# TensorE's warm-up in a table-lookup and ranking kernel: 56 one-column products and 10 of 512 columns instead of 13 of 512

## What is computed

```python
e = jnp.stack([tbl_0[ids[:, 0]], ..., tbl_25[ids[:, 25]]], axis=1)        # 512 x 26 x 128
combined = jnp.concatenate([dense[:, None, :], e], axis=1)                # 512 x 27 x 128
interactions = jnp.einsum('bnd,bmd->bnm', combined, combined)
z = jnp.concatenate([dense, interactions[:, _TRIU_I, _TRIU_J]], axis=1)   # 128 + 351
h = jnp.concatenate([z, dense], axis=1)
h = jnp.maximum(h @ W_top1 + b_top1, 0.0)                                 # 607 -> 512
h = jnp.maximum(h @ W_top2 + b_top2, 0.0)                                 # 512 -> 256
y = h @ W_top3                                                            # 256 -> 1
```

## Time and profile before

| what | before |
|---|---|
| runs, median (lowest to highest) | 102.37 us (102.18 to 102.53) |
| the profiled execution | 101.98 us |
| its span, first to last instruction | 100.2 us |
| PE busy | 94.5 us, 1525 products and 1525 weight loads |
| DVE / ACT / POOL busy | 53.2 / 48.1 / 60.5 us |
| the chain that ended last | PE 69%, DVE 20%, DMA 3%, ACT 3%, issue 2% |
| the warm-up, L474 | 13 products, 1.2 to 6.3 us |

### The profile page before, as it was taken

One profiled execution on the slowest core, in us unless ns is written; L12 is line 12 of the kernel. 1 busy time (PEld: TensorE's weight loads), 2 busy tenths in 40 slices (PEclk: granted clock), 3 DMA queues, 4 the chain that ended last, 5 costly groups with the idle time before them and its releaser, 6 DMA issues.

```text
span 100.2 us, 3476 instructions
## 1 busy us (share of the span) xinstructions
PE 94.5 (94%) x1525; PEld 78.4 (78%) x1525; DVE 53.2 (53%) x118; ACT 48.1 (48%) x82; POOL 60.5 (60%) x66
## 2 busy tenths in 40 slices
PE   5999997999999999999999999999999999998990
PEld 1358765778888888899989978899988979987970
DVE  4599999999999979927000250226002701026020
ACT  2844999299399579747310325006240444003521
POOL 1488777777777878767777777777777760000000
DMA  2899999999999999981212212122221220000000
GB/s 62 237 333 245 242 238 257 241 232 232 256 241 241 244 233 259 380 316 48 59 52 59 59 52 62 52 59 52 59 59 52 59 52 26 7 7 0 7 0 1
DMA packets 5365, 13.46 MB, mean 134 GB/s; under 512 B 1731, under 2 KB 1991, under 8 KB 5222
## 3 DMA queue, kind: packets, MB, share of 16 engines
q1 hardware_dynamic: 3260, 9.11, 35.4%
q0 software_dynamic: 1920, 3.94, 15.5%
q10 hardware_dynamic: 170, 0.18, 0.7%
HBM read 13.23 MB, written 0.00 MB: 132 GB/s over the span
## 4 chain that ended last, share of the span: by engine, by line
PE 69%; DVE 20%; DMA 3%; ACT 3%; issue 2%; DVEq 0%
PE ps_a L337 30%; DVE onehot L573 12%; PE ps_gram L374 12%; PE ps_a L423 9%; PE ps_h L437 5%; PE ps_rows L352 5%; DVE part_sb L582 4%; PE ps_a L400 3%; DMA idrow<-ids_by_table 3%; DVE table_sb L600 2%; DVE z L605 2%; PE ps_h L466 1%; PE ps_rows L449 1%; PE ps_z L385 1%; ACT xt L694 1%
## 5 line engine op out<-in xcount | busy, mean ns | idle before, releaser
L310 POOL DMA_INDIRECT rows_sb<-tbl,ids_sb x60 | 60.0, 1000 | 20.9 <-issue 16.8
L337 PE MATMUL ps_a<-onehot,part_sb 125*128 125x512 f32 (+1 forms) x208 | 45.0, 367 | 0.8 <-DVE part_sb L582 0.5
L337 PEld LDWEIGHTS ps_a<-onehot,part_sb 125*128 125x128 f32 x208 | 34.7, 190 | 7.9 <-DVE part_sb L582 1.7
L573 DVE TENSOR_SCALAR onehot<-idrow,row_id 125x1024 fp32r<-125x1024 int16 (+1 forms) x42 | 27.9, 716 | 2.2 <-DMA idrow<-ids_by_table 1.7
L582 DVE TENSOR_TENSOR part_sb<-table_sb,part_sb 125x512 fp32r<-125x512 f32 x22 | 14.4, 677 | 2.3 <-ACT part_sb L666 2.3
L687 ACT COPY xt<-ps_a 128x512 f32<-128x512 f32 (+1 forms) x13 | 7.5, 579 | 14.8 <-PE ps_a L337 14.8
L374 PE MATMUL ps_gram<-xt 128*27 128x27 f32 x1024 | 13.2, 195 | 0.3
L694 ACT COPY xt<-ps_rows 128x512 f32<-128x512 f32 (+3 forms) x17 | 9.9, 588 | 7.3 <-PE ps_rows L352 7.3
L374 PEld LDWEIGHTS ps_gram<-xt 128*27 128x27 f32 x1024 | 11.0, 107 | 3.0 <-ACT xt L694 0.6
L666 ACT CAST part_sb<-table_sb 125x1024 fp32r<-125x1024 f32 (+1 forms) x12 | 11.7, 984 | 2.7 <-DMA table_sb<-tbl 2.7
L636 DVE TENSOR_SCALAR table_sb<-ps_a,columns_sb 128x128 f32<-128x128 f32 x8 | 2.4, 346 | 18.9 <-PE ps_a L423 15.7
(11 more groups left out here) (41 smaller groups left out, 43.5 us busy)
## 6 DMA issues: line engine op xcount, KB each, us to landing
table_sb<-tbl SPq DMA_DIRECT2D x11, 448.0 KB
idrow<-ids_by_table SPq DMA_DIRECT2D x5, 256.0 KB, 8.5
w_sb<-w SPq DMA_DIRECT2D x1, 1280.0 KB, 11.9
rows_sb<-tbl,ids_sb POOLq DMA_INDIRECT x60, 6.6
table_sb<-tbl SPq DMA_DIRECT2D x10, 52.0 KB
w_sb<-w SPq DMA_DIRECT2D x1, 512.0 KB, 10.8
dense_sb<-dense_by_column SPq DMA_DIRECT2D x1, 256.0 KB, 9.0
idrow<-ids_by_table ACTq DMA_DIRECT2D x1, 128.0 KB, 2.9
```

The costliest lines, as they stand in the source:

```text
L310: pool.indirect_dma_start(rows_sb[:, t % ROWS_RING, k, :], None, tables[f], bass.IndirectOffsetOnAxis(ids_sb[:, t, f:f + 1], 0),).then_inc ...
L337: last = pe.matmul(ps_a[:, i % 2, a:b], parts_sb[part][:, w, c * D:(c + 1) * D], unit_onehot(u, c)[:, member, a:b], start=(part == HIGH an ...
L573: dve.tensor_scalar(unit_onehot(u, c), idrow[0:VP, w, 0:n, :], row_id[0:VP, first + c:first + c + 1], None, ALU.is_equal).then_inc(onehot_ ...
```

## The change

The warm-up constant becomes 10, and 56 products of one column on one column of weights are issued in front of it. Nothing else is changed: the lookups and all that follows stand 106 instructions later in TensorE's program (56 x 2 more, 3 x 2 fewer). The results of both loops are overwritten later, as before.

```diff
-WARM_UP = 13
+WARM_UP = 10
+SMALL = 56
...
             pe.wait_ge(zeros_ready, 1)
+            for _ in range(SMALL):
+                pe.matmul(ps_z[0:1, 0, 0:1], zeros[:, 0:1], zeros[:, 0:1], start=True, stop=True)
             for _ in range(WARM_UP):
                 pe.matmul(ps_z[:, 0, :], zeros[:, 0:P], zeros[:, :], start=True, stop=True)
```

## The result

The changed kernel takes 103.53 us in the median of 6 runs (102.56 to 104.08); the kernel before, run beside it on the same chip, takes 102.27 us (101.57 to 102.53). The ratio is 1.0118, with a 95% interval of 1.0076 to 1.016: slower by 1.2%, where the prediction had 101.8 us and called faster the likeliest. The profiled execution took 104.08 us, the longest of the six, for a span of 102.3 us.

What follows compares the result with a forecast made beforehand. VectorE was taken to bound the kernel until 20.40 us, then TensorE, with instruction-fetch stops late. Terms -0.73 + 0.10 + 0.05 = -0.58 us from the 102.37 us median gave 101.8 us, range 101.3 to 102.9; faster had 0.55.

Steps and rivals of the forecast that it cites:

- What bounds the kernel, and what a stop is: TensorE bounds from 20.40 us; it stops wherever it uses up a 256-instruction block faster than the next is fetched, 3.6 us.
- The 3.6 us that I called the measured minimum: At every block border: time from entering a block to the next being usable, 1.1 + 1.1 + 1.4 us.
- The stop among the L400 products: Between first and second L400 product, near 91 us: the 0.46 us stop goes, -0.73 us, bounds -0.46 and -0.84.
- The stop in the last gram stretch: Gram products from 87.82 us: a stop of 0.2 to 0.5 us instead of 0.28, +0.1, bounds -0.1 and +0.25.
- Earlier borders move into other stretches: Block borders from 50 to 80 us: each has more than 3.6 us in front, so no new stop, 0.
- the fixed delay from border to packet: At every block border: the next block's instruction packet starts about 1.1 us after TensorE enters the block.
- The fetch near 38 us: Instruction fetch amid table and weight transfers: ready by 48 us, before its block is wanted at 50; cost 0, bound +1.
- The warm-up: Before the first lookup: 56 small products at 33 ns, three large ones fewer, net +0.05 us, bounds 0 and +1.2.
- The 0.56 us that I let the clock give back: First lookup product, now starting as the clock level rises: no longer pays 0.56 us for the low level.
- Dear small products: Rival, before lookup 0: small products cost 55 ns each, lookup 0 ends 1.2 us later, result 102.9 us; chance 0.12.
- The clock rises later: Rival, first lookups: one-column products don't count as work, level rises at 8.9 us, +0.9 us, result 102.7; chance 0.15.
- The stop only moves: Rival: a border hits another short stretch or the late fetch holds gram up, taking back 0.5 to 0.7 us; chance 0.18.

Runs made afterwards that it cites:

- shifted by 192: Against the kernel before: 7 large and 102 small warm-up products instead of 13 large, +192 instructions for all that follows; 102.54 us, ratio 1.0037.
- shifted by 256: Against the kernel before: 5 large and 136 small warm-up products instead of 13 large, +256 instructions, one whole block; 103.34 us, ratio 1.012.

## Why the prediction was wrong

**What bounds the kernel, and what a stop is: held in kind, not in its number.** Blocks of 256 instructions in packets of 16 KB stand, and the stops after 85 us end at totals of 193 + 256 k in every kernel. The 3.6 us that I called the measured minimum is none. In the trace that I had, TensorE had executed 2443 products and loads, 2497 with the waits, by 84.96 us:

```profile
0.00:84.96 84.96, 82.28 (x1221) 67.82 (x1222) 49.61 (x103) 44.76 (x70) 60.45 (x66) 1.00 0.62 158
```

and it restarted at 2753 at 88.23, 3.27 us later. In the kernels shifted by 192 and 256 the block behind 2753 was in use 3.0 us after that border, with next to no stop (86.74 to 89.75 and 86.25 to 89.30 us, products 0.02 and 0.06 us apart at the crossing). The part that varies is the one from the border to the packet, which I took as 1.1 us throughout. That holds where TensorE has just restarted after a stop (1.1 to 1.2 us in the changed kernel and the one before). Elsewhere the packet starts mostly between 0.2 us before TensorE has executed the border (82.57 us for one executed at 82.81, with 53 small products behind the lookups) and 1.5 us after it, and in a few places over 2 us after it. From the start of a packet to use there are at least 2.2 us (87.19 to 89.40 with 64 small products, 87.53 to 89.75 shifted by 192). The Trainium skill ("Runtime: NRT & Kernel Launch", Instruction fetch mechanics) has crossing a block mostly hidden; late stops of 0.25 to 1.64 us in seven traces say otherwise where a block is used up by products 10 ns apart. The measurement decides.

**The stop among the L400 products, -0.73: held.** It went, and the products follow one another without a break. In the chain the four of them take 91.04 to 92.39 = 1.35 us before and 0.62 us after, which is 0.73 us less.

**The stop in the last gram stretch, "+0.1": too small.** I gave 0.2 to 0.5 us for it, counting 3.6 us from a border that TensorE passes at 85.3 to 85.6. The stop is 0.66 us, since that border itself was reached only at the end of another stop, at 87.86, and 87.86 + 3.8 = 91.68. Where the other stop is absent (64 small products) this one is 0.04 to 0.12 us in the chain, less than I gave, since 3.6 us was too long.

**"Earlier borders move into other stretches; from 50 to 80 us each has more than 3.6 us in front by my count … so 0": this step failed.** The count ended at 80 us, and the border that mattered lies behind it: what I called 2647 in the old program, whose block was asked for one block earlier, at old 2391, at 82.94 us. From there to 2647 are 4.9 us as it ran, and TensorE was ready after about 3.1 (at 86.03). By my own rule of 3.6 us that was a stop of 0.5 us, had I done the count. It was 1.64 because the packet left 2.2 us after its border and not 1.1: the second thing that the prediction had wrong is the fixed delay from border to packet. With the packet in time (64 small products; the last gathers left out) the stop is not there at all. The term of the sum is +1.6 instead of 0. What made the packet late is open. That the request waits while TensorE's program stands in a semaphore wait behind the border fits the changed kernel, its repetition and one place in the trace of before, where it costs nothing (the border at 59.65 us, a wait passed at 60.3, the packet at 61.46); it doesn't fit the border 449 of that same trace, or the packets that were in time with the same waits behind them.

**The fetch near 38 us, 0: held.** It moved at 42 us, the stretch from 50 us on starts at 49.97 us (49.74 before), and no stop is seen there.

**The warm-up, +0.05: held in its sum, not in its parts.** The timeline of PE in the changed kernel, from the start:

```profile
1.19 1.54 PE L475 MATMUL ps_z<-zeros 128*1 128x1 bf16 x56 [1.19 <-DVE zeros L560]
2.66 4.08 PE L477 MATMUL ps_z<-zeros 128*128 128x512 bf16 x10
6.39 2.86 PE L338 MATMUL ps_a<-onehot,part_sb 125*128 125x512 f32 x11
```

56 small products take 2.57 - 1.19 = 1.38 us from the first start to the last, 25 ns each, where I took 33 and bounded with 10 and 55. The first lookup product starts at 6.39 us, 0.03 later than before. The 0.56 us that I let the clock give back was read wrongly: at 0.43 us a product the low level costs 0.21 us more than 0.22, and the rest of the 0.78 us between the first two lookup products lies in the recorded start of the first, 0.07 us behind that of the last warm-up product (6.29), which has 0.43 us to run. In the changed kernel the second lookup product starts at 6.82 us, in its repetition at 7.33, before at 7.14; the 48th is at 18.92 in both and at 19.05 before. The Trainium skill ("TensorE: Matmul & The Clock Gate", Wait — 56ns, not 53.3ns?) gives about 25 ns as the floor between starts however few the columns; the trace agrees for these, with 512 columns 0.43 us apart right behind them, the low level. It does not hold for products spread over four column groups, which start about 10 ns apart in gram and 8 ns apart with one column.

**The rivals.** Dear small products: refuted, 25 ns. The clock rises later: seen, but without a price. Read by the distance of 512-column products (0.43 or 0.23 us), the higher level is there from the second lookup product on (6.82 us) in the first profile of the changed kernel, and only from 7.8 us on in its repetition; the 48th lookup product starts at 18.92 us in both. With 64 small products it came by 7.5 us in one execution and near 8.3 in the other. In the kernel with 102 small and 7 large products six lookup products stand 0.43 us apart from 7.20 us on and the level rose near 9.5 us, in the one with 136 small and 5 large ones near 8.4. So the moment scatters, and these rows don't say what it waits for. The stop only moves: this is the rival that came true, and I gave it the right place in words ("a border lands on another short stretch") and the wrong price. 0.5 to 0.7 us back was to give 102.2 to 102.6; the two stops are 2.3 us, and for a loss of over 1 us I had a chance of 0.03.

## What to carry to other kernels

Where an engine runs short instructions, mark its block borders through the whole program and count, for every border, the time to the next; an edit that adds instructions at the front is an edit to all of them, and a count that leaves out 5 us is no count. Don't take the smallest distance between two stops for the smallest that there is: look for borders that were passed without a stop too. Look then at what stands right behind each border: a semaphore wait there can go with a fetch that is late by over a microsecond, and 16 instructions more ahead of it took that away here. Keep the first border out of the time in which the first loads are awaited: the three kernels that had it there were the latest in front. Before pricing a stop that goes, look at what lands just behind it: here the last gather had 0.3 us to spare in the kernel before.

## What the runs showed of the hardware that I had not expected

- The packet of the next block can be late, and then it starts 1.0 to 1.2 us after a semaphore wait is passed: in the changed kernel and its repetition (waits passed at 84.1 and 83.5, packets at 85.14 and 84.60), once in the kernel before (60.3 and 61.46), in the kernel shifted by 256 (50.3 and 51.34), and in the one shifted by 192, where the border was passed at 79.2, a wait 51 instructions behind it at 81.85, and the packet came at 82.90, at no cost. It is not a fixed distance, and the wait does not decide it alone: in the kernel with 53 small products behind the lookups the same waits stood in the same places and the request got away in time; with 98 small products over four groups, the same shift by 192, the packet came at 79.87, 1.0 us after the border; and in the kernel before one came at 48.46 in the middle of a wait. That a wait holds the request is argued from these times; what decides whether it gets out first is open.
- From 60 us on, gathers with no 16 KB instruction packet beside them took 2.4 to 2.6 us from issue to landing (2.55 for the last one of the changed kernel, whose packet came after it). With one beside them many took as long, but all that took 2.7 us or more had one: 3.8 us in the kernels with 53 small products behind the lookups and with 98 over four groups, 3.0 and 2.9 us in the two executions with 64.
- In the three traces with a packet of instructions in the first 5 us, ScalarE's waits for the table loads are 3.9 to 4.5 us in total, and the 48th lookup product starts 1.1 to 1.3 us later than before. In the others the waits are 2.5 to 3.2 us, but 4.2 us in one, so the packet is a likely cause and not a shown one.
- One-column products start 25 ns apart in one column group and 8 ns apart spread over four (the first at 1.19, the 98th at 1.92 us).
